# Column pairs in the simple recurrence, gate biases written by ScalarE, a new deal of the shared expert's tiles, in a four-layer recurrent kernel

## The chip, the cores and the metric

The kernel runs on one core of one Trainium2 chip. The metric is device time in microseconds, the median of several executions of the whole kernel. Before the change it is 1193.13 us (three runs, 1192.58 to 1193.31). Below, TensorE is PE in the rows of the profile, its weight loads are PEld, VectorE is DVE, ScalarE is ACT, GpSimd is POOL, and SyncE is SP (SPq for its queue of transfers).

## The reference

Four layers run in a row on x of shape (16, 256, 256), that is batch B, time T, width D. Each layer's output is added to its input. Only the first three matter here.

```python
# layer 0: a simple recurrence, h0 = cond
xW = einsum('ntd,dh->tnh', x, Wx) + b
h  = tanh(h @ Wh + xW[t])                      # for each of 256 times
x  = x + hs
# layer 1: an LSTM, h0 = cond, c0 = 0
hb = x[:, t] @ Wx + b + h @ Wh                 # 4 x 256 wide: i, f, o, g
c  = sigmoid(f) * c + sigmoid(i) * tanh(g)
h  = sigmoid(o) * tanh(c)
x  = x + hs
# layer 2: a shared expert for all, and two of four experts for each batch entry
x  = x + gelu(x @ sw1 + sb1) @ sw2 + sb2 + (routed experts, weighted)
# layer 3: a low-rank adapter, with weights made from cond
x  = x + adapter(x, cond)
```

## The kernel before

**Layout.** Activations are kept transposed: 128 partitions hold half of the width (C = 2 halves), the free dimension holds batch and time. Each product is done to nearly float32 accuracy with float16 operands: a value is split into a high part (HI) and a low part (LO), and three matmuls per pair of 128-blocks are summed in PSUM (helper `three`, lines 1132 to 1134): high weight times high data, low weight times high data, high weight times low data.

**Blocks and steps.** Time is cut into NB = 16 blocks of U = 16 steps. `block_steps(it, ...)` is written out once per engine. In block `it`, step `u` does the LSTM of time it*16+u, the simple recurrence of the next block at the same place, and a part of the shared expert for the block before (FILL, a table of tiles h, hidden, and d, down). So three layers run at the same time, one block apart. Before block 0 the simple recurrence runs alone for 16 steps. In blocks 1 to 8 (`matrix=True`) an eighth of the expert weights is split into high and low parts on the way (`weight_hi` on ACT, line 483; `weight_lo` on DVE, line 680; at the steps EXPERT_WINDOWS), and a part of the adapter's matrix is made (`low_rank` on PE, `low_hi` line 579 on ACT, `low_lo` line 902 on DVE, both in steps 14 and 15). After block 15 follow the routed experts and the adapter, which the change leaves almost alone.

**One step on PE.** First the LSTM's 48 matmuls of 16 columns (24 and 12 for the gates f, i, g, then 8 and 4 for o; lines 1229 and 1235). They wait for the state's high part (`v_hh`), and the last 12 of the first set for its low part (`v_hl`). Then the simple recurrence: 8 matmuls on the high part of its state (line 1203), 4 on the low part (line 1209). Then the input products of later steps for the LSTM: `fig_x` (64 columns) and `o_x` (128 columns), each tile with a bias matmul (line 1285) ahead of six others. Then the tiles that FILL names. At the end of a block `rnn_x`, 14 matmuls of 256 columns (line 1187 is its bias).

**One step on ACT.** `lstm_gates` (tfig, line 523, waits for f, i, g; to, line 527), then `rnn_step` (rf and RH, lines 517 and 518, the same tanh written as float32 and float16), then `lstm_cell` (tc, line 534), then the gelu of a hidden tile if the step has one (line 539), then the weight splits.

**One step on DVE.** `lstm_step`: fc, ig, c2 (lines 790, 791, 793), cell (795), then after tc the state's high part hh (797), h2 (800), the low part hl (802), and X (804). Then the longer work: `split_x2` (747, 750, 754), `split_g` (the cast at 777 and the difference at 779 for each gelu), `weight_lo`, and `split_x` (737 and 740), which makes the input XR of the simple recurrence two blocks ahead.

**One step on POOL.** The low part of the simple recurrence's state (line 396), and its sum with x (398 to 407).

Every engine takes its instructions in the order written here, and semaphores join them. The order is written by hand, nothing is planned at run time.

Of the kernel before, what the change touches and what calls it, by code (L numbers as in the profile page):

```python
# [22 lines left out]
ALU = mybir.AluOpType  # L23
# [34 lines left out]
def build_program(nc, a, out, scratch):  # L58
    ctx = ExitStack()
    with ctx:  # L60
# [25 lines left out]
        ones_pad = sb("ones_pad", [P, 256], F16)  # L86
        idf = sb("idf", [P, P], F32)
# [7 lines left out]
        rf = sb("rf", [P, 2, C, B], F32)  # L95
        x1s = sb("x1s", [P, 2, C, B], F32)
# [6 lines left out]
        cell = sb("cell", [P, C * B], F32)  # L103
# [52 lines left out]
        def late(*shape):  # L156
# [41 lines left out]
            a_xr p_xr pe_rx pe_r a_rh  p_rlo p_x1 p_x1h p_x1l  # L198
            pe_fig pe_o a_fig v_ig v_c2 a_tc v_hh v_h2 v_hl v_x2
# [37 lines left out]
        EXPERT_WINDOWS = (2, 4, 6, 8, 10, 12, 13, 14)  # L237
# [46 lines left out]
        def _(sp):  # L284
            with nc.allow_non_contiguous_dma(reason="small tables, once"):
# [22 lines left out]
                for quarter in range(4):  # L308
                    load_x(1, quarter)
                small_tables(sp)  # L310
# [68 lines left out]
        def _(pool):  # L379
# [9 lines left out]
            def rnn_step(blk, r):  # L389
# [80 lines left out]
        def _(act):  # L470
# [23 lines left out]
            nc.scalar.activation(XR[:, HI, 0].rearrange("p t b -> p b t"), X[:, 0, :, 0:U], ACT.Copy  # L494
# [40 lines left out]

            def gelu(tile, m, scale, bias, banks):
# [4 lines left out]


            piece = 0
            for r in range(U):
                rnn_step(0, r)
                for _ in range(LSTM_PIECES[r]):
# [5 lines left out]
            def block_steps(it, first, last, matrix=False):  # L552
                for u in range(U):
                    lstm_gates(it, u)
                    if not last:
                        rnn_step(it + 1, u)
                    lstm_cell(it, u)
                    if not first:
                        for kind, m in FILL[u]:
                            if kind == "h":  # L560
                                gelu(it * M + m, m, 1 / S_W1, sb1[:, m:m + 1], HB)
# [28 lines left out]
            for m in range(M):  # L590
                gelu(NB * M + m, m, 1 / S_W1, sb1[:, m:m + 1], HB)
# [63 lines left out]
        def _(dve):  # L655


            dve.sem_inc(s["v_gh"], M)
# [32 lines left out]
            V.memset(cell[:], 0.0).then_inc(s["v_const"], 1)  # L691
# [865 lines left out]
```

## Time and profile before

| what | value |
|---|---|
| median of 3 runs | 1193.13 us |
| the profiled execution's own time | 1185.64 us |
| its span, first to last instruction | 1183.8 us |
| PE busy, PEld busy | 1137.6 us (96%), 1028.1 us (87%) |
| DVE, ACT, POOL busy | 885.1 us (75%), 513.6 us (43%), 401.2 us (34%) |
| mean granted clock of TensorE | 0.968 of full speed |
| recurrences: block 0 to block 15 | from 50.6 us to 757.6 us of the span |

A row of the timeline gives an instruction's start and its duration, both in us. The durations of neighbours on one engine overlap, so what an instruction takes up of its engine's time is read as the distance between two starts where the second waits for nothing else. Busy time of PE is not PE at its peak, since matmuls are pipelined.

### The profile page before, as it was taken

Reading aid. Unit: us, or ns where it says so; the run is one execution under the profiler, and the core shown is the slowest. Engines: PE = TensorE matmul, PEld = TensorE weight load, DVE = VectorE, ACT = ScalarE, POOL = GpSimd, SP = SyncE. Lnnn points to the kernel's source line nnn. Section 1 sums busy time; section 2 is a strip of 40 time slices with the busy share of each in tenths; the row PEclk is TensorE's granted clock in tenths of the full one; section 3 lists DMA queues with packets and bytes.
Section 4 is the critical chain, followed back from the end, with each engine's and each line's share of the span. In section 5 each row is a group of like instructions: output and inputs, shape, how many; then the busy total and the mean of one; then the engine's idle time right before and its main releaser. Section 6 shows DMA issues by size and latency. Waiting matters only on the chain.

```text
span 1183.8 us, 58924 instructions
## 1 busy us (share of the span) xinstructions
PE 1137.6 (96%) x24138; PEld 1028.1 (87%) x24138; DVE 885.1 (75%) x3368; ACT 513.6 (43%) x1897; POOL 401.2 (34%) x1369
## 2 busy tenths in 40 slices
PE   4899999999999999999999999899999999999898
PEld 3789889889889899999999998778888888888777
DVE  6577888887887887787787778787666666666697
ACT  3344444454444444444444443433333333333476
POOL 2654454454454454554454441064000000000041
PEclk7758999999999999999999999899999999999999
DMA  8211202202112021110000000000000000000022
GB/s 244 74 39 44 79 5 80 71 13 79 29 54 80 11 73 26 16 16 11 4 4 5 4 4 4 2 1 2 2 2 2 1 2 2 2 2 2 3 77 86
DMA packets 43282, 37.17 MB, mean 31 GB/s; under 512 B 23128, under 2 KB 38794, under 8 KB 43020
## 3 DMA queue, kind: packets, MB, share of 16 engines
q1 hardware_dynamic: 42412, 33.12, 9.2%
q8 instruction: 197, 3.23, 1.1%
q14 instruction: 65, 0.53, 0.1%
q10 hardware_dynamic: 608, 0.30, 0.1%
HBM read 28.42 MB, written 4.98 MB: 28 GB/s over the span
## 4 chain that ended last, share of the span: by engine, by line
PE 86%; DVE 8%; ACT 2%; POOL 2%; issue 2%; DMA 1%; SPq 0%; POOLq 0%; DVEq 0%; ACTq 0%
PE bank L1132 17%; PE bank L1133 17%; PE bank L1134 17%; PE bank L1229 16%; PE bank L1235 8%; PE bank L1203 4%; PE bank L1209 2%; DVE seq L740 2%; PE bank L1285 1%; ACT tc L534 1%; DVE LH L797 1%; PE bank L1275 1%; PE bank L1500 1%; DMA XHL<-in_x 1%; PE bank L1472 1%
## 5 line engine op out<-in xcount | busy, mean ns | idle before, releaser
L1229 PE MATMUL bank<-LH,seq 128*128 128x16 f16 x8192 | 282.1, 170 | 12.3 <-DVE LH L797 10.7
L1229 PEld LDWEIGHTS bank<-LH,seq 128*128 128x128 f16 x8192 | 250.6, 96 | 44.0 <-DVE LH L797 32.1
L539 ACT ACTIVATE gel<-bank,seq 128x256 f32<-128x256 f32 x256 | 121.2, 474 | 215.7 <-PE bank L1134 215.5
L1132 PE MATMUL bank<-XHL,WE 128*128 128x256 f16 x768 | 210.3, 274 | 2.6 <-DVE XHL L763 2.1
L1132 PE MATMUL bank<-GH,WE 128*128 128x256 f16 x768 | 209.8, 273 | 2.6 <-DVE GH L779 2.3
L777 DVE CAST GH<-gel 128x256 f16<-128x256 f32 x384 | 123.6, 322 | 117.6 <-ACT gel L539 110.8
L1134 PE MATMUL bank<-XHL,WE 128*128 128x256 f16 x768 | 210.4, 274 | 0.0
L1133 PE MATMUL bank<-XHL,WE 128*128 128x256 f16 x768 | 210.3, 274 | 0.0
L1133 PE MATMUL bank<-GH,WE 128*128 128x256 f16 x768 | 209.7, 273 | 0.0
L1134 PE MATMUL bank<-GH,WE 128*128 128x256 f16 x768 | 209.6, 273 | 0.0
L523 ACT ACTIVATE tfig<-bank 128x96 f32<-128x96 f32 x256 | 63.8, 249 | 286.4 <-PE bank L1235 286.4
L1235 PE MATMUL bank<-LH,seq 128*128 128x16 f16 x4096 | 177.2, 169 | 1.6 <-issue 1.6
L779 DVE TENSOR_TENSOR GH<-gel,GH 128x256 f16<-128x256 f32 x384 | 168.2, 438 | 13.2
L396 POOL TENSOR_TENSOR RH<-rf,RH 128x32 f16<-128x32 f32 x256 | 64.1, 250 | 322.8 <-ACT RH L518 313.0
L1134 PE MATMUL bank<-seq 128*128 128x64 f16 (+2 forms) x960 | 145.5, 206 | 0.0
L1133 PE MATMUL bank<-seq 128*128 128x64 f16 (+2 forms) x960 | 144.6, 206 | 0.0
L1132 PE MATMUL bank<-seq 128*128 128x64 f16 (+2 forms) x960 | 143.7, 206 | 0.0
L1235 PEld LDWEIGHTS bank<-LH,seq 128*128 128x128 f16 x4096 | 139.1, 96 | 1.1 <-issue 1.1
L462 POOL TENSOR_TENSOR seq<-X,seq 128x512 f16<-128x512 f32 x16 | 21.8, 1367 | 336.1 <-ACT seq L600 336.1
L790 DVE SCALAR_TENSOR_TENSOR fc<-tfig,cell 128x32 f32<-128x32 f32 x256 | 52.1, 204 | 73.0 <-ACT tfig L523 69.6
L405 POOL TENSOR_TENSOR seq<-x1s,seq 128x32 f16<-128x32 f32 x256 | 86.3, 337 | 36.7
L407 POOL COPY X<-x1s 128x32 f32<-128x32 f32 x256 | 93.8, 366 | 0.3
(190 smaller groups left out, 2583.9 us busy)
## 6 DMA issues: line engine op xcount, KB each, us to landing
stage<-in_L_cond_ew SPq DMA_DIRECT2D x8, 1024.0 KB, 8.7
stage<-in_L_cond_W SPq DMA_DIRECT2D x8, 1024.0 KB, 6.1
XHL<-in_x SPq DMA_DIRECT2D x8, 512.0 KB, 9.0
out<-WE SPq DMA_DIRECT2D x16, 256.0 KB, 2.2
stage<-in_L_cond_sw SPq DMA_DIRECT2D x2, 1024.0 KB, 5.4
scratch<-rows SPq DMA_DIRECT2D x96, 8.0 KB, 2.3
stage<-in_L_cond_Wx SPq DMA_DIRECT2D x1, 1024.0 KB, 8.7
stage<-in_L_cond_Wh SPq DMA_DIRECT2D x1, 1024.0 KB, 10.8
```

The lines of the kernel that those rows point to most:

```text
L396: nc.gpsimd.tensor_tensor(RH[:, slot, LO], rf[:, slot], RH[:, slot, HI], ALU.subtract).then_inc(s["p_rlo"], 1)
L405: nc.gpsimd.tensor_tensor(xs[:, LO, :, r % G, :], x1s[:, slot], xs[:, HI, :, r % G, :], ALU.subtract).then_inc(s["p_x1l"], 1)
L407: nc.gpsimd.tensor_copy(x, x1).then_inc(s["p_x1"], 1)
L523: nc.scalar.activation(tfig[:], FIG[u // H % 2][:, 0:6 * H * B].rearrange("p (m t b) -> p m t b", m=6, t=H)[:, :, u % H, :], ACT.Tanh, sca ...
L539: nc.scalar.activation(gel[:, m % 2, :], banks[m % len(banks)][:, 0:256], ACT.Gelu_apprx_tanh, scale=scale, bias=bias).then_inc(s["a_g"], 1)
L777: V.tensor_copy(GH[:, m % 4, HI], gel[:, m % 2]).then_inc(s["v_gh"], 1)
L779: V.tensor_tensor(GH[:, m % 4, LO], gel[:, m % 2], GH[:, m % 4, HI], ALU.subtract).then_inc(s["v_gl"], 1)
L1132: MM(out_, w(HI), x(HI), start=start, stop=False, skip_group_check=True)
L1133: MM(out_, w(LO), x(HI), start=False, stop=False, skip_group_check=True)
L1134: return MM(out_, w(HI), x(LO), start=False, stop=stop, skip_group_check=True)
L1229: MM(z, LW[:, h, 1, c, tile * P:(tile + 1) * P], LH[:, old, HI, c], start=False, stop=False, skip_group_check=True)
L1235: last = MM(z, LW[:, HI, 1, c, tile * P:(tile + 1) * P], LH[:, old, LO, c], start=False, stop=(c == C - 1), skip_group_check=True)
```

## The change

- **Simple recurrence.** The bank RB is laid out anew: two groups of 8 steps follow each other in it, with two columns sets (a = 0 and 1) for each. High weights meet the pair of high and low state in one matmul of 32 columns, so a step has 4 matmuls of 16 columns and 4 of 32 columns in place of 12 of 16. A DVE reduction (`rnn_sum`, into the new tile rz) adds the two sets, and stands in `lstm_step` behind hl. ACT's rf and RH wait for it. `rnn_x` is done for 8 steps at a time, with matmuls of 128 columns, in steps 0 and 8.
- **Biases.** After the first two turns no bias matmul precedes `fig_x` and `o_x`. ACT writes the biases into PSUM (`seed`, 384 elements for f, i, g after each fourth step; 256 for o after each eighth) from a small table that eight more transfers load and POOL scales.
- **ACT's order.** tc comes before rf and RH; then seeds, gelu, the high part of XR (`x_hi`, formerly DVE's cast), weight splits.
- **Gelu.** ACT computes it twice, once as float32 (gel) and once as float16 (GH, HI). DVE's cast goes, and only the difference (`shared_lo`) stays.
- **XR.** It is read across and written along (before: read along, written across). X_HI = (9, 10) on ACT, X_LO = (10, 12) on DVE.
- **DVE.** The scaling into cell goes, c2 is kept and scaled inside the next product.
- **Deal.** FILL is dealt in halves of a tile, the number per step being HALVES. The tiles come ahead of `fig_x` in a step. `o_x` for the second half of a block is in steps 3 and 5. EXPERT_WINDOWS and SPLIT_WINDOWS move.

```diff
-        EXPERT_WINDOWS = (2, 4, 6, 8, 10, 12, 13, 14)
+        EXPERT_WINDOWS = (2, 3, 4, 5, 6, 8, 9, 11)
...
 # ACT
             def rnn_step(blk, r):
                 n = blk * U + r
-                z = RB[:, :].rearrange("p (m t b) -> p m t b", m=C, t=U)[:, :, r, :]
-                act.wait_ge(s["pe_r"], n + 1)
+                z = rz[:]
+                act.wait_ge(s["v_rz"], n + 1)
...
+            def seed(n_read, bank_, tiles, steps, done):
+                act.wait_ge(s["a_tc"], n_read)
+                n = (tiles.stop - tiles.start) * steps * B
+                act.wait_ge(s["p_gate_bias"], 3)
+                nc.scalar.activation(bank_[:, 0:n].rearrange("p (m t) -> p m t", t=steps * B),
+                                     gate_bias[:, tiles].rearrange("p (m o) -> p m o", o=1).to_broadcast(
+                                         [P, tiles.stop - tiles.start, steps * B]), ACT.Copy).then_inc(s[done], 1)
+            def seeds(it, u, last):
+                if u % H == H - 1 and not (last and u >= U - 2 * H):
+                    seed(it * U + u + 1, FIG[u // H % 2], slice(0, 6), H, "a_fig_seed")
+                if u % G == G - 1 and not last:
+                    seed(it * U + u + 1, OB[u // G], slice(6, 8), G, "a_o_seed")
+            def x_hi(blk, c):
+                act.wait_ge(s["pe_rx"], 2 * blk)
+                nc.scalar.activation(XR[:, HI, c], X[:, c, :, blk * U:(blk + 1) * U].rearrange("p b t -> p t b"),
+                                     ACT.Copy).then_inc(s["a_xr"], 1)
+            def shared_gelu(tile, m):
+                act.wait_ge(s["pe_h"], tile + 1)
+                act.wait_ge(s["v_gl"], tile - 1)
+                nc.scalar.activation(gel[:, m % 2, :], HB[m % 2][:, 0:256], ACT.Gelu_apprx_tanh,
+                                     scale=1 / S_W1, bias=sb1[:, m:m + 1])
+                act.wait_ge(s["pe_d"], tile - 3)
+                nc.scalar.activation(GH[:, m % 4, HI], HB[m % 2][:, 0:256], ACT.Gelu_apprx_tanh,
+                                     scale=1 / S_W1, bias=sb1[:, m:m + 1]).then_inc(s["a_g"], 1)
...
                 for u in range(U):
                     lstm_gates(it, u)
+                    lstm_cell(it, u)
                     if not last:
                         rnn_step(it + 1, u)
-                    lstm_cell(it, u)
+                    seeds(it, u, last)
...
 # DVE
+            def shared_lo(tile, m):
+                dve.wait_ge(s["a_g"], tile + 1)
+                V.tensor_tensor(GH[:, m % 4, LO], gel[:, m % 2], GH[:, m % 4, HI], ALU.subtract
+                                ).then_inc(s["v_gl"], 1)
+            def rnn_sum(n):
+                pair = RB[:, :].rearrange("p (a m t b) -> p m t b a", a=2, m=C, t=G)[:, :, n % G]
+                dve.wait_ge(s["pe_r"], n + 1)
+                V.reduce_sum(rz[:], pair, AX_X).then_inc(s["v_rz"], 1)
...
-                V.tensor_tensor(c2[:], fc[:], ig[:], ALU.add).then_inc(s["v_c2"], 1)
-                dve.wait_ge(s["v_c2"], n + 1)
-                V.tensor_scalar(cell[:], c2[:], 0.5, None, ALU.mult)
+                V.scalar_tensor_tensor(c2[:], fc[:], 0.5, ig[:], ALU.mult, ALU.add).then_inc(s["v_c2"], 1)
...
                 V.tensor_tensor(hl, h2[:], hh, ALU.subtract).then_inc(s["v_hl"], 1)
+                if rnn:
+                    rnn_sum(n + U)
...
 # PE
+                if r % G == 0 and n > 0:
+                    rnn_x(blk, r // G)
...
                 for m in range(C):
                     for c in range(C):
-                        for h in (HI, LO):
-                            MM(z[:, m, r], RW[:, h, 1, c, m * P:(m + 1) * P], RH[:, old, HI, c],
-                               start=False, stop=False, skip_group_check=True)
+                        MM(z[:, 0, m, r % G], RW[:, LO, 1, c, m * P:(m + 1) * P], RH[:, old, HI, c],
+                           start=False, stop=False, skip_group_check=True)
...
-                        last = MM(z[:, m, r], RW[:, HI, 1, c, m * P:(m + 1) * P], RH[:, old, LO, c],
+                        last = MM(z[:, :, m, r % G], RW[:, HI, 1, c, m * P:(m + 1) * P], RH[:, old, :, c],
                                   start=False, stop=(c == C - 1), skip_group_check=True)
...
-FILL = [[] for _ in range(U)]
-for _m in range(M):
-    FILL[max(2 * _m - 1, 1)].append(("h", _m))
-    FILL[min(2 * _m + 2, 14)].append(("d", _m))
+HALVES = [0, 3, 2, 2, 2, 2, 2, 3, 0, 3, 2, 3, 2, 3, 2, 1]
+O_STEPS = (3, 5)
...
+X_HI, X_LO = (9, 10), (10, 12)
-SPLIT_WINDOWS = (0, 0, 2, 12)
+SPLIT_WINDOWS = (0, 0, 3, 7)
```

The new FILL takes the halves in the order h0, then h1, d0, h2, d1, up to h7, d6, then d7. So a hidden tile is finished, and its gelu done, in steps 1, 2, 4, 6, 7, 10, 11 and 13.

## Rows read from the trace of the kernel before

**Rows 1.** The page: busy time by engine, its share of the span, instructions.

```profile
PE 1137.6 (96%) x24138; PEld 1028.1 (87%) x24138; DVE 885.1 (75%) x3368; ACT 513.6 (43%) x1897; POOL 401.2 (34%) x1369
```

**Rows 2.** Windows of blocks 0, 1, 9, 15: PE, PEld, DVE, ACT, POOL, clock, DMA.

```profile
50.60:95.30 44.70, 41.17 (x1175) 38.34 (x1173) 30.56 (x148) 19.14 (x96) 22.85 (x80) 0.58 0.14 42
95.30:140.90 45.60, 45.16 (x1311) 41.53 (x1309) 37.20 (x163) 22.03 (x97) 21.39 (x80) 1.00 0.08 27
...
460.90:504.00 43.10, 43.10 (x1273) 40.70 (x1270) 33.28 (x154) 18.45 (x88) 20.78 (x80) 1.00 0.13 15
...
717.80:757.60 39.80, 35.87 (x981) 31.53 (x978) 32.38 (x169) 13.51 (x53) 0.00 (x0) 1.00 0.02 3
```

**Rows 3.** Timeline of PE in block 8: start us, duration us, operation.

```profile
424.90 0.19 PE L1134 MATMUL bank<-seq 128*128 128x64 f16 x1
424.93 0.27 PE L1132 MATMUL bank<-XHL,WE 128*128 128x256 f16 x1
425.04 0.27 PE L1133 MATMUL bank<-XHL,WE 128*128 128x256 f16 x1
...
425.66 0.76 PE L1229 MATMUL bank<-LH,seq 128*128 128x16 f16 x24
426.27 0.45 PE L1235 MATMUL bank<-LH,seq 128*128 128x16 f16 x12
```

**Rows 4.** Timeline of ACT and DVE, the same step of block 8.

```profile
424.31 0.25 ACT L523 ACTIVATE tfig<-bank 128x96 f32<-128x96 f32 x1 [1.19 <-PE bank L1235]
424.59 0.19 DVE L790 SCALAR_TENSOR_TENSOR fc<-tfig,cell 128x32 f32<-128x32 f32 x1 [0.35 <-ACT tfig L523]
...
425.41 0.19 DVE L797 SCALAR_TENSOR_TENSOR LH<-to,tc 128x32 f16<-128x32 f32 x1
...
425.82 0.19 DVE L802 TENSOR_TENSOR LH<-h,LH 128x32 f16<-128x32 f32 x1
425.93 0.21 DVE L804 SCALAR_TENSOR_TENSOR X<-h,X 128x32 f32<-128x32 f32 x1
...
426.71 0.42 DVE L779 TENSOR_TENSOR GH<-gel,GH 128x256 f16<-128x256 f32 x1
426.75 0.25 ACT L523 ACTIVATE tfig<-bank 128x96 f32<-128x96 f32 x1 [0.49 <-PE bank L1235]
...
427.05 0.18 DVE L790 SCALAR_TENSOR_TENSOR fc<-tfig,cell 128x32 f32<-128x32 f32 x1
```

**Rows 5.** Timeline of ACT: pairs in which the second waits for nothing else.

```profile
452.13 0.47 ACT L539 ACTIVATE gel<-bank,sb 128x256 f32<-128x256 f32 x1 [0.41 <-PE bank L1134]
452.50 0.41 ACT L483 ACTIVATE WE<-stage 128x256 f16<-128x256 f32 x1
...
455.89 1.33 ACT L579 ACTIVATE rows<-low_f 128x256 f16<-128x256 f32 x1 [1.13 <-DVE low_f L896]
456.73 0.70 ACT L483 ACTIVATE WE<-stage 128x256 f16<-128x256 f32 x1
...
1165.25 0.62 ACT L600 ACTIVATE seq<-X 128x512 f16<-128x512 f32 x1
1165.77 0.65 ACT L635 ACTIVATE WE<-bank 128x256 f32<-128x256 f32 x2
```

**Rows 6.** Timeline of ACT's tfig in block 9: steps 3, 4, 15, next block.

```profile
469.28 0.25 ACT L523 ACTIVATE tfig<-bank 128x96 f32<-128x96 f32 x1 [1.48 <-PE bank L1235]
471.73 0.25 ACT L523 ACTIVATE tfig<-bank 128x96 f32<-128x96 f32 x1 [0.50 <-PE bank L1235]
...
499.99 0.25 ACT L523 ACTIVATE tfig<-bank 128x96 f32<-128x96 f32 x1 [2.16 <-PE bank L1235]
504.01 0.25 ACT L523 ACTIVATE tfig<-bank 128x96 f32<-128x96 f32 x1 [2.95 <-PE bank L1235]
```

**Rows 7.** Groups by line and shape, whole span: count, busy us, mean ns.

```profile
L740 DVE TENSOR_TENSOR seq<-X,seq 128x256 f16<-128x256 f32 x30 | 39.0, 1299 | 0.0
...
L754 DVE TENSOR_REDUCE blocksum<-X 128x16 f32<-128x256 f32 x32 | 13.0, 411 | 0.0
```

More of the change, by code:

```diff
@@ L309, in _ @@
                     load_x(1, quarter)
+                for i, tile in enumerate(FIG_TILES + O_TILES):
+                    sp.dma_start(gate_bias[:, i:i + 1], a["L1_cond_b"][tile * P:(tile + 1) * P].rearrange("(p o) -> p o", o=1)
+                                 ).then_inc(s["ld_gate_bias"], 16)
                 small_tables(sp)
@@ L821, in _ @@
             for r in range(U):
+                rnn_sum(r)
                 for _ in range(LSTM_PIECES[r]):
@@ L913, in block_steps @@
                                 split_x2(it - 1, k)
-                        for kind, m in FILL[u]:
-                            if kind == "h":
-                                split_g(it * M + m, m)
+                        for kind, m, halves in FILL[u]:
+                            if kind == "h" and C - 1 in halves:
+                                shared_lo(it * M + m, m)
                     for i in SHARED_PIECES[u] if first else ():
@@ L1237, in lstm_step, with hidden, down_, shared_hidden @@
                     last.then_inc(s[done], 1)
[L1239 to L1242 removed]
+            def hidden(tile, w, x, bank_, free, halves=range(C)):
+                if 0 in halves:
+                    free()
+                for c in halves:
                     last = three(bank_[:, 0:256], lambda h: w(h, c), lambda h: x(h, c), c == 0, c == C - 1)
[L1244 to L1249 removed]
+                if C - 1 in halves:
+                    last.then_inc(s["pe_h"], 1)
+            def down_(tile, j, w, first, last_, ybank, halves=range(C)):
+                if 0 in halves:
+                    pe.wait_ge(s["v_gl"], tile + 1)
+                for c in halves:
                     last = three(ybank[:, c * 256:(c + 1) * 256], lambda h: w(h, c),
                                  lambda h: GH[:, j % 4, h], first and c == 0, last_)
[L1252 to L1254 removed]
+                if C - 1 in halves:
+                    last.then_inc(s["pe_d"], 1)
+            def shared_hidden(blk, m, halves=range(C)):
                 tile = blk * M + (M + m)
@@ L1353, in spread_logits, with block_steps @@
                    skip_group_check=True).then_inc(s["pe_gate"], 1)
-            def block_steps(it, first, last, rx, matrix=False):
+            def block_steps(it, first, last, matrix=False):
                 for u in range(U):
@@ L1363, in block_steps @@
                         logits()
+                    if not first:
+                        for kind, m, halves in FILL[u]:
+                            if kind == "h":
+                                shared_hidden(it - 1, m, halves)
+                            else:
+                                shared_down(it - 1, m, halves)
                     if u == 0:
@@ L1514, in _, with fill_table @@
             adapter_steps(pe, step)
-FILL = [[] for _ in range(U)]
-for _m in range(M):
-    FILL[max(2 * _m - 1, 1)].append(("h", _m))
-    FILL[min(2 * _m + 2, 14)].append(("d", _m))
+HALVES = [0, 3, 2, 2, 2, 2, 2, 3, 0, 3, 2, 3, 2, 3, 2, 1]
+O_STEPS = (3, 5)
+def fill_table():
+    jobs = [("h", 0)] + [job for m in range(1, M) for job in (("h", m), ("d", m - 1))] + [("d", M - 1)]
+    stream = [(kind, m, c) for kind, m in jobs for c in range(C)]
+    table, at = [], 0
+    for n in HALVES:
+        step = {}
+        for kind, m, c in stream[at:at + n]:
+            step.setdefault((kind, m), []).append(c)
+        table.append([(kind, m, tuple(cs)) for (kind, m), cs in step.items()])
+        at += n
+    assert at == len(stream)
+    return table
+FILL = fill_table()
 N_SCRATCH = 16 * Q * C * 3 * 4
```

171 lines of the change are left out of this document (80 added, 91 removed).

## The prediction

> **What bounds the kernel now.** I read the page first, then windows by block, then the timeline inside one step. The page has PE busy for 96% of the span [rows 1], and the windows show where that is so: block 9 is PE from end to end, 43.1 of 43.1 us, while DVE has 33.3 us of work in it and ACT 18.4 [rows 2]. ACT looks free.
>
> The starts of neighbouring matmuls give PE's prices at the full clock: 24 matmuls of 16 columns take 0.61 us, so 0.025 each; one of 64 columns 0.03 (0.0285 over longer runs); one of 256 columns 0.11 [rows 3]. For 128 columns I take 0.056, half of the 256. A step of before costs PE 48 + 12 matmuls of 16 columns (1.50 us), plus for `fig_x` 0.20 per tile, plus 0.66 per tile of the shared expert. By that, steps 3, 5, 7 and so on with one hidden tile and one `fig_x` tile cost 2.35 us, and step 15 with `o_x`, `rnn_x` and a `fig_x` tile 1.50 + 0.20 + 0.78 + 1.53 = 4.0. The starts of tfig in block 9 show 2.45 for step 3 and 4.02 for step 15 [rows 6]. So the long steps are PE's work, and the short ones stand at 2.45, above PE's 2.35.
>
> That 2.45 is the second bound, the LSTM's own loop. From tfig, in one step: fc at 0.28, the state's high part at 1.10 to 1.29, its low part hl at 1.51, X at 1.62, PE's next LSTM matmuls at 1.35, next tfig at 2.44 [rows 3, 4]. A block of 16 steps can't be shorter than 16 x 2.44 = 39.0 us, whatever PE has to do.
>
> **The change on PE.** Matmuls of 32 columns: no row has one, it lies between 0.025 (16 columns) and 0.0285 (64), and I take 0.025. The simple recurrence falls from 12 to 8, 0.10 us a step, 1.6 a block (1.54 at the other bound). The bias matmuls that go are 6 x 4 of 64 columns and 4 of 128: 0.91 a block. `rnn_x` costs 28 x 0.056 = 1.57 in place of 14 x 0.11 = 1.53. With the new deal, PE's work W per step is 1.40, plus 0.78 for `rnn_x` in steps 0 and 8, plus 0.327 per half, 0.17 per `fig_x` tile, 0.33 per `o_x` tile. It comes out at 2.40 in the even steps 2, 4, 6, 10, 12, 14 and 2.52 to 2.57 in the others, 39.7 us a block, against 42.4 before (43.1 measured with the short steps raised to 2.45). In blocks 1 to 8 `low_rank` adds 1.14.
> The Trainium skill (TensorE: Matmul & The Clock Gate, Back-to-back issue gap) gives some 25 ns from start to start for anything up to 64 columns. The trace agrees at 16 columns with 0.025, and by the page 32 columns cost the same.
>
> **The change on ACT, step by step.** rf and RH now wait for `rnn_sum`, which stands behind hl on DVE. It starts where X started, 1.62 after tfig. It is a reduction of 64 elements to 32; the nearest rows are the 32-element operations at 0.19 [rows 4] and the reduction of 256 at 0.41 [rows 7], and I take 0.21. So rf can't start before 1.87. RH follows 0.09 later and whatever comes next 0.08 after that, at 2.05. All the rest that ACT has in the step, seeds, gelus, `x_hi`, weight splits, is queued behind it, and behind all that waits the next tfig, wanted at 2.44. From tc to 1.87 ACT stands idle with this work behind the waiting instruction. The room left for it is 0.39, or 0.50 where PE's W of 2.55 sets the step.
> The Trainium skill (PSUM — Partial Sum Buffer, Engine vs sequencer instructions) says that the queues of ScalarE and VectorE are strictly first in, first out. The trace agrees: ACT sits idle for 1.19 us ahead of a tfig [rows 4].
>
> What has to go into that room, as distances between starts: a gelu takes 0.37 [rows 5], and two of them 0.74; a copy of 256 elements takes between 0.27 and 0.37 there, 512 take 0.52 [rows 5], so I take 0.30 for a weight split or an `x_hi`, 0.40 for the seed of 384 elements (bounds 0.27 and 0.52) and 0.27 for the one of 256. `x_hi` reads across; the old layout, which wrote across, cost DVE 1.30 [rows 7], and that is its upper bound.
>
> A gelu step therefore makes the next tfig late by 0.74 - 0.39 = 0.35. DVE adds to it: `shared_lo` waits for the second gelu's end at 2.05 + 0.37 + 0.47 = 2.89, starts at 2.92 and gives DVE back 0.34 later (426.71 to 427.05 in [rows 4]) at 3.26, while fc is wanted at 2.79 + 0.28 = 3.07. Lateness 0.19 more. The next state is late by the sum, PE waits, and the interval that follows a gelu step is 2.44 + 0.35 + 0.19 = 2.98, where PE needs 2.40 or 2.55. Where the step before was PE's, at 2.55, it is 2.86.
>
> The intervals of steps 0 to 15 in blocks 9 to 14 by this rule, each the larger of W and 2.44 plus the lateness: 2.58, 2.55, 2.86, 2.97, 2.44, 2.97, 2.44, 2.97, 3.64, 2.55, 2.44, 3.39, 3.37, 2.55, 2.86, 2.57. Step 8 is the longest because step 7 has both seeds and a gelu pair, 0.40 + 0.27 + 0.74 = 1.41. Step 11 follows a gelu pair with `x_hi` (1.04) and `x_lo` behind it on DVE, step 12 a seed and a pair (1.14), step 0 both seeds. Sum 45.15 against 43.1: +2.05 a block.
>
> In blocks 1 to 8 each weight split adds 0.30 on ACT, and `weight_lo`, 0.34 on DVE, waits for it at the end of the queue. Four of the eight stand in gelu steps (2, 4, 6, 11). The same rule gives 3.29, 2.55, 2.86, 3.30, 2.92, 3.30, 2.56, 3.30, 3.64, 2.55, 2.72, 3.39, 3.70, 3.12, 2.44, 3.24 (step 15 follows `low_hi`, 0.84 by [rows 5]; steps 12 and 13 carry `low_rank`). Sum 48.9 against 45.6 [rows 2]: +3.3.
>
> **What costs nothing, and its cover.** The cast of gel, the cell product and the casts and scattered writes of XR leave DVE, some 9.6 us a block by its rows, and 16 reductions come (3.4): DVE has 33.3 of 43.1 us and was not the bound, so this gives nothing but shorter lateness, which is counted above. Eight transfers of 512 bytes stand ahead of the small tables in SP's queue; they are early in the kernel, the first load behind them waits for weight splits anyway, and if that cover failed they would cost 1 to 2 us once. POOL's three scalings fall between blocks, POOL has 20.8 of 43.1 us.
>
> **Start and end.** `rnn_x(1)`, 3 us at half clock, leaves the path before block 0, and `rnn_x(2)` its end, but 1.5 comes back in each stage, the 16 lone steps get the reduction (+0.25 less 0.12 of matmuls each) behind weight splits and copies on DVE, and block 0 (clock 0.58 [rows 2]) has seeds and `x_hi` in the way of tfig. I take +2.5 for both stages, between -4 and +8. Block 15 has no rf and RH, so ACT is free after tc: -0.8; in the tiles behind it eight casts less: -0.5.
>
> **The sum.** 8 x 3.3 = 26.4; 6 x 2.05 = 12.3; +2.5; -1.3. That is +39.9 us. The profiled execution took 1185.6 us with a span of 1183.8, the median of the three runs is 1193.1, 0.6% more; the sum is a difference of 1225.5 to 1185.6, and set upon the median it gives 1233.
>
> **Rivals.**
> *PE's work comes through.* If ACT's queue never holds up tfig (the sum of the pair is ready early, or the two gelus take less than half), the blocks go down to W: -3.4 in blocks 9 to 13, -1.9 in 14, -4.1 in 1 to 8 (their waits for loads stay), -3 at the start: about -55, 1138. For it: PE is at 96% and ACT at 43% [rows 1]. Against: rf's place behind hl and the gelus' place behind rf are in the program, and 0.74 doesn't fit in 0.39. It decides from the point where a pair and what stands with it take less than 0.4 to 0.5. The Trainium skill (Perfetto Trace Analysis, Identifying the Most-Contended Engine) would optimise the engine with the highest occupancy first, here PE with its weight loads at 87%; by that page alone this rival is the forecast. Chance 0.17.
> *Half hidden.* If the second gelu and the copies follow at 0.27, the lower bound of [rows 5], a pair overruns by 0.24, and each of eight intervals is 0.1 to 0.2 shorter, those with seeds and splits 0.3: 43.2 to 43.6 in blocks 9 to 14 and 46.5 to 47 in 1 to 8, so +10 to +15: about 1206. Chance 0.15.
> *The clock falls.* PE gets gaps of 0.4 to 0.6 us in seven or eight steps of a block and of 1 us in step 8, which has no tile. In block 0, without tiles, the granted clock was 0.58 [rows 2]. At half clock a step's tiles and input products would take twice their time, about +1 us a step in the stretches concerned; two steps a block in 14 blocks add 28: about 1260. Against it: block 15, PE busy for 35.9 of 39.8 us, kept 1.00 [rows 2]. Chance 0.08.
> *The forecast*, ACT's queue behind the pair sum: 0.60, with its own range 1216 to 1250.
>
> **How the numbers follow.** A measurement of this kernel tells some 0.2% from no change, 2.4 us. Faster comes from the first rival and a little of the second: 0.19. Slower: 0.76. Within 0.2%: 0.05, the lower edge of the second. The range of 8 in 10 leaves out the first rival and the far side of the clock's: 1190 to 1258.
>
> **What the changed profile would show.** The idle time ahead of rf is put down to DVE's reduction, about 0.8 us a step; tfig is no longer released by PE in about half of the steps; PE's wait for the state's high part (line 797 before) grows from some 0.1 to about 5 us a block; PE busy falls below 90% in blocks 1 to 14; the intervals of tfig alternate between 2.44 to 2.57 and about 3, with the longest, 3.6, after step 7. Block 9 takes 45 us, a matrix block 49. The prediction is wrong if tfig's intervals are all 2.4 to 2.57, if the reduction starts well before hl ends, or if two gelus start less than 0.3 apart.

## The result, and the profile after

The changed kernel takes 1261.34 us (median of 4 runs, 1258.69 to 1263.24) against 1193.22 us before (4 runs): ratio 1.0573, 95% interval 1.0555 to 1.0591. It is slower by 68 us, where 40 were forecast, and lies 3 us above the forecast's range. The profiled execution took 1259.87 us with a span of 1258.1 and a mean granted clock of 0.953.

The page of the kernel after, the line of engines (busy us, share, count), answers to [rows 1]:

```profile
PE 1135.2 (90%) x22906; PEld 1016.8 (81%) x22906; DVE 788.8 (63%) x3210; ACT 597.7 (48%) x2147; POOL 381.4 (30%) x1372
```

Every engine but ACT has no more work than before, and the span is longer. So the time went into waiting. The windows of blocks 0, 1, 9 and 15, same columns as [rows 2]:

```profile
53.60:101.00 47.40, 39.08 (x1111) 36.85 (x1108) 28.30 (x146) 23.23 (x105) 20.57 (x78) 0.57 0.12 40
101.00:151.60 50.60, 45.17 (x1213) 41.15 (x1211) 30.40 (x153) 27.01 (x115) 20.73 (x80) 0.95 0.10 31
508.00:554.90 46.90, 42.51 (x1191) 39.40 (x1189) 27.46 (x145) 23.38 (x106) 19.64 (x82) 1.00 0.12 15
787.90:826.80 38.90, 35.00 (x949) 31.79 (x949) 27.30 (x145) 17.12 (x64) 0.62 (x3) 0.99 0.01 4
```

Block 9 takes 46.9 us where it took 43.1, and PE is busy for 42.5 of it, not for all. Only block 15, which has no simple recurrence, is shorter, 38.9 against 39.8. The table of waits of the kernel after (engine, what waits, what for: us in total, times, longest):

```profile
ACT rf L525 <- DVE rz L832: 194.2, 256, 2.9
ACT tc L542 <- DVE c L847: 161.3, 256, 1.6
...
PE bank L1281 <- DVE LH L849: 78.3, 135, 1.6
...
ACT tfig L531 <- PE bank L1287: 38.6, 79, 3.7
```

and two rows of the same table of the kernel before:

```profile
ACT tfig L523 <- PE bank L1235: 286.4, 248, 5.3
...
PE bank L1229 <- DVE LH L797: 10.7, 32, 0.9
```

Before, ACT waited for PE at nearly every tfig. Now it does so 79 times, and PE waits for the state: 78 us in place of 11. What stands between is the first row, rf waiting for the pair sum in each of 256 steps. One gelu step of block 9, timeline of ACT, DVE and POOL (start, duration):

```profile
525.32 0.25 ACT L531 ACTIVATE tfig<-bank 128x96 f32<-128x96 f32 x1 [0.31 <-PE bank L1287]
...
525.52 0.26 POOL L404 TENSOR_TENSOR seq<-X,rf 128x32 f16<-128x32 f32 x1
525.61 0.22 DVE L844 SCALAR_TENSOR_TENSOR fc<-tfig,c 128x32 f32<-128x32 f32 x1 [0.84 <-ACT tfig L531]
...
525.92 0.24 POOL L409 TENSOR_TENSOR seq<-x1s,seq 128x32 f16<-128x32 f32 x1
525.97 0.25 DVE L847 SCALAR_TENSOR_TENSOR c<-fc,ig 128x32 f32<-128x32 f32 x1
...
526.84 0.19 DVE L854 TENSOR_TENSOR LH<-h,LH 128x32 f16<-128x32 f32 x1
526.95 0.22 DVE L832 TENSOR_REDUCE rz<-bank 128x32 f32<-128x64 f32 x1
...
527.20 0.23 ACT L525 ACTIVATE rf<-rz 128x32 f32<-128x32 f32 x1 [0.72 <-DVE rz L832]
527.34 0.21 ACT L526 ACTIVATE RH<-rz 128x32 f16<-128x32 f32 x1
527.46 0.46 ACT L575 ACTIVATE gel<-bank,sb 128x256 f32<-128x256 f32 x1
...
527.81 0.46 ACT L578 ACTIVATE GH<-bank,sb 128x256 f16<-128x256 f32 x1
...
528.17 0.25 ACT L531 ACTIVATE tfig<-bank 128x96 f32<-128x96 f32 x1
...
528.31 0.43 DVE L816 TENSOR_TENSOR GH<-gel,GH 128x256 f16<-128x256 f32 x1 [1.02 <-ACT GH L578]
```

This is the step of the forecast: the pair sum (rz) starts 1.63 after tfig; rf starts at 1.88, after ACT has stood idle for 0.72; the two gelus start at 2.14 and 2.49, and the next tfig at 2.85, with no wait of its own. A second thing wasn't forecast. c2 (the profile writes it c) takes 0.25 and fc 0.22, beside POOL's operations. Before the change fc took 0.19 [rows 4], and so did c2 in the same step of block 8, on the timeline of DVE:

```profile
424.92 0.19 DVE L793 TENSOR_TENSOR c<-fc,ig 128x32 f32<-128x32 f32 x1
```

The chain of tfig starts in block 13 shows what a pair of steps costs, steps 3 to 5 and the next:

```profile
703.48 0.25 ACT L531 ACTIVATE tfig<-bank 128x96 f32<-128x96 f32 x1
...
706.23 0.24 ACT L531 ACTIVATE tfig<-bank 128x96 f32<-128x96 f32 x1
...
709.07 0.25 ACT L531 ACTIVATE tfig<-bank 128x96 f32<-128x96 f32 x1
...
711.80 0.25 ACT L531 ACTIVATE tfig<-bank 128x96 f32<-128x96 f32 x1 [0.31 <-PE bank L1287]
```

The interval of a step runs here from its own tfig to the next one; the prediction's lists count the same interval under the step that it ends in. Steps 4 and 5, one with a gelu and one without, take 2.84 + 2.73 = 5.57. The whole block takes 46.43.

Where the time went, from the tfig starts of the two traces (the stages begin at 51.7, 96.3, 460.9, 717.8 before and at 53.6, 101.0, 508.0, 787.9 after): start stage +1.9, block 0 +2.8, blocks 1 to 8 +42.4, blocks 9 to 14 +23.0, block 15 -0.95, all behind it +5.1. The last lies in the final 89 us (84 before), where the granted clock was 0.92 against 0.98; no run tests it. The profiled executions differ by 74 us, the medians by 68, because the profiled execution before was 8 us faster than its median.

### The profile page after: what moved, and what is told of

The parts are those of the page before. It is cut to its first block and busy times, and to the rows that moved or that the text cites. A ratio compares the mean times of both kernels' runs of the same rounds, so it can differ in the third digit from the quotient of the medians.

```text
span 1258.1 us, 56828 instructions
## 1 busy us (share of the span) xinstructions
PE 1135.2 (90%) x22906; PEld 1016.8 (81%) x22906; DVE 788.8 (63%) x3210; ACT 597.7 (48%) x2147; POOL 381.4 (30%) x1372
## 5 line engine op out<-in xcount | busy, mean ns | idle before, releaser
L1281 PEld LDWEIGHTS bank<-LH,seq 128*128 128x128 f16 x8192 | 242.6, 96 | 113.4 <-DVE LH L849 105.9
L525 ACT ACTIVATE rf<-rz 128x32 f32<-128x32 f32 x256 | 58.7, 229 | 194.2 <-DVE rz L832 194.2
L1183 PE MATMUL bank<-seq 128*128 128x64 f16 (+1 forms) x1024 | 148.7, 205 | 0.0
L1182 PE MATMUL bank<-seq 128*128 128x64 f16 (+1 forms) x1024 | 147.4, 205 | 0.1
L1181 PE MATMUL bank<-seq 128*128 128x64 f16 (+1 forms) x1024 | 145.9, 205 | 0.6 <-POOL seq L409 0.6
L823 DVE CAST GH<-gel 128x256 f16<-128x256 f32 x256 | 78.3, 306 | 104.0 <-ACT gel L569 103.1
L1287 PEld LDWEIGHTS bank<-LH,seq 128*128 128x128 f16 x4096 | 139.4, 96 | 0.0
L542 ACT ACTIVATE tc<-c 128x32 f32<-128x32 f32 x256 | 58.7, 229 | 161.3 <-DVE c L847 161.3
L470 POOL TENSOR_TENSOR seq<-X,seq 128x512 f16<-128x512 f32 x16 | 19.2, 1205 | 342.3 <-ACT seq L644 342.3
L1181 PEld LDWEIGHTS bank<-seq 128*128 128x128 f16 x1024 | 99.7, 101 | 3.5 <-POOL seq L409 0.7
```

Of the source, the lines that this page charges most:

```text
L525: nc.scalar.activation(rf[:, r % 2], z, ACT.Tanh, scale=1 / S_RNN)
L542: nc.scalar.activation(tc[:], c2[:], ACT.Tanh, scale=0.5).then_inc(s["a_tc"], 1)
L823: V.tensor_copy(GH[:, m % 4, HI], gel[:, m % 2]).then_inc(s["v_gh"], 1)
L1181: MM(out_, w(HI), x(HI), start=start, stop=False, skip_group_check=True)
L1182: MM(out_, w(LO), x(HI), start=False, stop=False, skip_group_check=True)
L1183: return MM(out_, w(HI), x(LO), start=False, stop=stop, skip_group_check=True)
```

## The experiments

The kernel before was run on the same chips: 1191.38 us in the first group of four runs below, 1191.69 in the second, 1190.36 in the third, 1188.97 in the last three. Ratios are to it. The kernel before varies by some 4 us between these chips and that of the first measurement (1188.97 to 1193.22), so a small difference to the changed kernel's 1261.34 us is better read from the ratios.

**1. The sum ahead of the state.** `rnn_sum` moves on DVE from behind hl to between c2 and hh.

```diff
                 V.scalar_tensor_tensor(c2[:], fc[:], 0.5, ig[:], ...)
+                if rnn:
+                    rnn_sum(n + U)
                 dve.wait_ge(s["a_tc"], n + 1)
...
                 V.tensor_tensor(hl, h2[:], hh, ALU.subtract)
-                if rnn:
-                    rnn_sum(n + U)
```

> The changed kernel with one thing moved: DVE does the pair sum between c2 and the state's high part, where it waits for tc anyway. Queue theory (rf and RH late behind hl, everything else of ACT late behind them): rf starts about 1.1 us after tfig in place of 1.89, the room for seeds, gelus and splits grows from 0.39 to about 1.2 us, tfig is again released by PE in nearly every step, blocks 9 to 13 fall from 46.6 to about 40 us, blocks 1 to 8 from 50.8 to about 42, in all about 1261 - 100 = 1160, faster than before (1193). Rival (ACT's added work is too much wherever it stands, or the sum delays the state): blocks stay above 43 us, 1200 to 1250. Second rival (the reductions in steps 0 and 8 hold up the state because PE does rnn_x ahead of the recurrence): two steps a block 0.3 us longer, 9 us in all of the gain.

1172.89 us, ratio 0.9844 (0.9817 to 0.9871): 88 us less than the changed kernel, and 1.6% faster than the one before. The blocks fell less than expected, 9 to 14 to 41.3 us on average (expected 40) and 1 to 8 to 45.0 (expected 42), so the 1160 expected wasn't reached. One gelu step of its block 13, timeline:

```profile
632.95 0.25 ACT L531 ACTIVATE tfig<-bank 128x96 f32<-128x96 f32 x1 [0.87 <-PE bank L1287]
...
633.67 0.22 DVE L832 TENSOR_REDUCE rz<-bank 128x32 f32<-128x64 f32 x1
...
633.92 0.23 ACT L525 ACTIVATE rf<-rz 128x32 f32<-128x32 f32 x1
...
634.53 0.46 ACT L578 ACTIVATE GH<-bank,sb 128x256 f16<-128x256 f32 x1
...
635.39 0.25 ACT L531 ACTIVATE tfig<-bank 128x96 f32<-128x96 f32 x1 [0.40 <-PE bank L1287]
```

rf starts at 0.97 in place of 1.88, the gelu pair is over at 2.04, and tfig waits for PE again, as it does 187 times in this run. The place of one operation of 0.22 us decides the sign of the change.

**2. One gelu.** DVE casts gel again, ACT computes one gelu.

```diff
+                V.tensor_copy(GH[:, m % 4, HI], gel[:, m % 2]).then_inc(s["v_gh"], 1)
...
-                nc.scalar.activation(GH[:, m % 4, HI], HB[m % 2][:, 0:256], ACT.Gelu_apprx_tanh, ...)
```

> The changed kernel with one gelu per tile on ACT and the cast back on DVE. If the second gelu is the cause by itself: each of eight intervals a block 0.5 us shorter, about 1261 - 50 = 1210. Queue theory: ACT's part goes (0.37 fits in the room of 0.39), but the cast and the difference on DVE now follow the late gelu, end 0.4 to 0.5 us after fc is wanted and take its place; only 0.05 to 0.1 us a gelu step is won, 1248 to 1256.

1259.53 us, ratio 1.0583 (1.0554 to 1.0613), no change; not even the small gain expected came. ACT's lateness of 0.35 went, and DVE's cast took its place, as its timeline shows:

```profile
705.83 0.30 DVE L815 CAST GH<-gel 128x256 f16<-128x256 f32 x1 [0.65 <-ACT gel L575]
706.16 0.43 DVE L817 TENSOR_TENSOR GH<-gel,GH 128x256 f16<-128x256 f32 x1
706.59 0.19 DVE L845 SCALAR_TENSOR_TENSOR fc<-tfig,c 128x32 f32<-128x32 f32 x1
```

tfig had started at 705.74, so fc comes at 0.85, not 0.28. Behind a late rf the work holds up the loop on whichever engine it stands.

**3. POOL later.** POOL waits for the next c2 before its last four operations of a step.

```diff
+                if n >= U:
+                    pool.wait_ge(s["v_c2"], n - U + 2)
```

> The changed kernel with one more wait on POOL: after the low part of the simple recurrence's state it waits for the next LSTM step's c2 before its four other operations, which nothing needs soon. All intervals of tfig are 0.1 us longer than the 2.44 of the loop before, in steps without any work of ACT too; in block 15, where POOL does nothing, they are 2.44. Contention theory (POOL's operations now run beside fc and c2, before they ran beside h2): fc falls from 0.218 to 0.19 us, c2 from 0.25 to 0.19, the shortest intervals from 2.63 to 2.55, 1.3 us a block, about 1261 - 18 = 1243. Rival (the longer loop is the form of c2 and the added wait ahead of fc): nothing changes or it gets slower, 1260 or more.

1273.84 us, ratio 1.069 (1.0658 to 1.0722), slower. fc, ig and c2 did fall to 0.19, and the step behind a gelu from 2.73 to 2.64. But x's sum now comes late for PE's input products at the start of each block, and they stand ahead of the LSTM's matmuls. The timeline of PE:

```profile
712.85 0.20 PE L1183 MATMUL bank<-seq 128*128 128x64 f16 x1 [0.84 <-POOL seq L411]
```

The interval of step 0 grew from 2.48 to 3.28. So the time of this run can't decide for or against the contention, and the gain of 18 us expected didn't come.

**4. Cell product back on DVE.** c2 is the plain sum again, and the scaling into cell returns.

```diff
-                V.scalar_tensor_tensor(c2[:], fc[:], 0.5, ig[:], ALU.mult, ALU.add)
+                V.tensor_tensor(c2[:], fc[:], ig[:], ALU.add)
+                V.tensor_scalar(cell[:], c2[:], 0.5, None, ALU.mult)
```

> The changed kernel with the cell product back on DVE, c2 a plain sum again and no wait ahead of fc. Rival of the contention theory: the loop falls by 0.1 us a step, about 1240. Contention theory: fc, ig and c2 keep their longer durations, the cell product stands where DVE waits for tc, so within 3 us of 1261.

1263.72 us, ratio 1.0597 (1.0561 to 1.0633), no change, and fc and c2 stay long. Their new form isn't the cause.

**5. Biases on PE.** No seeds on ACT, the bias matmuls return.

```diff
-                    seeds(it, u, last)
```

> The bias matmuls stand on PE again and ACT's seeds are gone; the sum of the pair stays behind hl. Theory (ACT's queue behind the pair sum holds up tfig): the interval after step 7 falls from 3.77 to about 3.05, step 11's from 3.3 to 2.9, step 15's from 2.85 to about 2.65, and PE's extra 0.91 us a block falls mostly into its gaps. That is -1.2 to -1.4 us a block in 15 blocks: about 1241 us (1236 to 1246). Rival (PE's work sets the blocks, the seeds are hidden in ACT's idle time): +0.5 to +0.9 a block, 1269 to 1275 us.

1240.68 us, ratio 1.0417 (1.0393 to 1.0442), 19 to 21 us less, as the theory had it. A seed behind a late rf costs more than the bias matmuls that it saves.

**6. rf and RH last on ACT.** The sum stays behind hl. ACT does seeds, gelus, copies and splits first.

```diff
                     lstm_cell(it, u)
-                    if not last:
-                        rnn_step(it + 1, u)
                     seeds(it, u, last)
...
+                    if not last:
+                        rnn_step(it + 1, u)
```

> ACT does rf and RH after the seeds, the gelu pair, the copy of XR and the weight splits; the sum of the pair stays behind hl on DVE. Theory (what costs is work queued behind the waiting rf, not the sum's place in itself): a gelu pair starts at about 1.2 after tfig and is over at 1.95, rf then starts where its sum lets it anyway, and tfig comes on time. The intervals fall to 2.54 to 2.65, the one after step 7 to 2.8: blocks 9 to 14 to about 42.3 us, the kernel to about 1195 us (1180 to 1210). Rival (the sum's place behind hl, so the late state of the simple recurrence, costs by itself, or two gelus are too much for ACT anywhere): 1240 us or more.

1189.23 us, ratio 0.9973 (0.9956 to 0.9991): 72 us back without touching DVE. Timeline of ACT in its block 13:

```profile
645.07 0.25 ACT L531 ACTIVATE tfig<-bank 128x96 f32<-128x96 f32 x1 [0.31 <-PE bank L1287]
...
646.14 0.46 ACT L575 ACTIVATE gel<-bank,sb 128x256 f32<-128x256 f32 x1
646.49 0.47 ACT L578 ACTIVATE GH<-bank,sb 128x256 f16<-128x256 f32 x1
646.95 0.23 ACT L525 ACTIVATE rf<-rz 128x32 f32<-128x32 f32 x1
...
647.61 0.25 ACT L531 ACTIVATE tfig<-bank 128x96 f32<-128x96 f32 x1 [0.31 <-PE bank L1287]
```

rf is no earlier than in the changed kernel (1.88), yet the next tfig, 2.54 after the first, waits for PE and for nothing on ACT. So it is not the late state of the simple recurrence that cost, but what stood behind the waiting instruction. The Trainium skill (PSUM — Partial Sum Buffer, Engine vs sequencer instructions) calls these queues strictly first in, first out; runs 1 and 6, which change an order and nothing else, agree with 88 and 72 us. (The prediction's own sign for it, ACT idle for 1.19 ahead of a tfig, shows a wait and not yet an order.) Run 6 stays 16 us behind run 1, 15 of them in blocks 1 to 8 (375.3 us against 360.1); what costs them wasn't tested.

**7. Early sum and biases on PE**, the edits of 1 and 5.

> The sum of the pair between c2 and the state (as in the run with 1172.9 us), and the biases on PE again. With the queue free PE is what is left: its 0.91 us a block come back, less some 0.2 at steps 7 and 8 where the seeds still held ACT: +0.7 a block in 15 blocks, about 1183 us (1179 to 1188). If the seeds on ACT are worth nothing also now: 1172 us. If they cost more than the matmuls: below 1170 us.

1179.26 us, ratio 0.9888 (0.9864 to 0.9912). With the queue free the seeds are worth 5 to 6 us, little more than the noise (the intervals of this run and run 1 just overlap); with it blocked they cost 19 to 21.

**8. Early sum and one gelu**, the edits of 1 and 2.

> The sum of the pair between c2 and the state, and one gelu with DVE's cast again. The cast (0.34 us) starts behind X at about 1.75 after tfig and the difference is over at about 2.5, ahead of the next fc at 2.72; ACT was idle anyway. So no change against 1172.9 us: 1170 to 1176. If DVE's time is what the second gelu buys: 1180 us or more.

1175.66 us, ratio 0.9855 (0.9807 to 0.9902), the same as run 1 within the intervals. The second gelu buys nothing that these runs tell.

**9. No pairs.** 12 matmuls of 16 columns, no sum, rf and RH read PE's bank; all else as changed.

```diff
-                z = rz[:]
-                act.wait_ge(s["v_rz"], n + 1)
+                z = RB[...][:, 0, :, r % G]
+                act.wait_ge(s["pe_r"], n + 1)
```

> All of the change but the column pairs: 12 matmuls of 16 columns again, no sum on DVE, rf and RH read PE's bank. Theory (the whole loss comes from rf waiting behind DVE's sum): rf starts at about 0.9 to 1.1 after tfig, the gelu pair and the seeds fit, and the blocks fall to PE's work, which is 0.10 us a step more than with pairs: blocks 9 to 14 at 41.3 to 42 us, about 1185 us (1178 to 1192). Rival (the second gelu, the seeds or the new deal cost by themselves): 1220 us or more.

1177.50 us, ratio 0.9882 (0.9848 to 0.9917). All of the change but the pairs gains; the pairs with their sum behind hl turn that into the loss of 68. Against run 1 the pairs are worth only about 5 us, within the intervals. Two parts are hidden in that: the first tfig comes at 46.5 without pairs and at 53.6 in run 1, and from there to the last tfig it is 700.8 us without them and 690.3 in run 1. So the pairs gain some 10 us in the blocks and lose some 7 ahead of them.

**10. Small POOL.** From block 0 on POOL's last four operations of a step cover one column each, so this kernel leaves out the rest of the simple recurrence's sum with x.

```diff
+                    nc.gpsimd.tensor_tensor(x1[:, one], x[:, one], h[:, one], ALU.add)
...
-                nc.gpsimd.tensor_tensor(x1, x, h, ALU.add)
```

> The kernel after the change with the four later operations of POOL's step cut to one column each from block 0 of the LSTM on (x1s, both parts of seq, X), so the sum of the simple recurrence with x is left out for all but that column. Theory (the loop of 2.54 in place of 2.44 is DVE's fc, ig and c2 slowed beside POOL's operations): fc, ig and c2 take 0.18 to 0.19 again, the steps after a gelu step fall from 2.73 to 2.64 and blocks 9 to 14 from 46.4 to 45.0 us: about 1238 us (1234 to 1243). Rival (the 0.1 us is from something else, such as the new order of ACT or the new form of c2): 1257 us or more.

1247.45 us, ratio 1.0475 (1.0438 to 1.0513): 14 us less than the changed kernel (12 by the ratios), between the two theories. Groups by line of the kernel after (total us, mean ns of one), then of this one:

```profile
L844 DVE SCALAR_TENSOR_TENSOR fc<-tfig,c 128x32 f32<-128x32 f32 x256 | 54.3, 212 | 56.4 <-ACT tfig L531 53.7 <-issue 1.2
...
L847 DVE SCALAR_TENSOR_TENSOR c<-fc,ig 128x32 f32<-128x32 f32 x256 | 52.6, 206 | 8.8
```

```profile
L859 DVE SCALAR_TENSOR_TENSOR c<-fc,ig 128x32 f32<-128x32 f32 x256 | 49.2, 192 | 8.9
...
L856 DVE SCALAR_TENSOR_TENSOR fc<-tfig,c 128x32 f32<-128x32 f32 x256 | 48.0, 187 | 59.6 <-ACT tfig L543 58.1 <-issue 1.2
```

The durations fall as expected, and steps 4 and 5 of block 13 take 2.75 + 2.65 = 5.40. The prediction's rule gives 2.79 + 2.63 = 5.42 for such a pair. So with the contention gone the rule is right to 0.02 for this pair. From fc to tc it is now 0.54 to 0.57 in nearly every step. But the block takes 45.47, not 45.0, and block 4 49.63 where 48.9 was forecast.

**11. Early sum, even deal.** HALVES = [0, 4, then twelve times 2, 4, 0].

> The sum of the pair between c2 and the state, and the shared expert's halves dealt as before the change: 0, 4, twelve times 2, 4, 0. PE's work by the prices of the prediction grows in step 8 by 0.65, in step 14 by 0.60 and in step 1 by 0.32, and falls in steps 7, 9, 11, 13, 15 by 0.10 each to the loop: +1.1 us a block in 15 blocks, about 1189 us (1180 to 1195). Rival (the deal does not matter, gaps take it up): 1173 us.

1178.02 us, ratio 0.9897 (0.9861 to 0.9934). The deal is worth 5 us of the 16 expected, and the intervals of this run and run 1 overlap. A block of the late ones takes 41.8 against 41.0. Step 14 grew by 0.62 as expected, but step 8 by 0.30 and not by 0.65, since in run 1 it stood above PE's work already (2.67).

**12. Early sum, later seed.** The seed for o moves from steps 7 and 15 to steps 8 and 0.

> The sum of the pair between c2 and the state, and the seed of 256 elements for o one step later, in the steps 0 and 8, which have no gelu. Theory (ACT's queue is what still holds up tfig after steps 7 and 15): the intervals of steps 7, 8 and 0 fall by 0.1 to 0.25 each, 0.5 us a block, about 1166 us (1162 to 1170). Rival (PE sets these steps): 1172 us.

1169.12 us, ratio 0.9809 (0.9773 to 0.9846). The interval of step 7 fell from 2.66 to 2.56, that of step 8 rose from 2.67 to 2.76, and blocks 10 to 14 take the same 41.0 as in run 1. The difference to run 1 is within the intervals, and the 0.5 us a block expected didn't come: the rival, that PE sets these steps, fits.

**13. Lone steps without pairs**, on top of 12: in the 16 steps ahead of block 0, 12 matmuls of 16 columns and no sum.

> The kernel with the early sum and the later seed, but in the 16 lone steps of the simple recurrence 12 matmuls of 16 columns and rf and RH straight from PE's bank, as in the run without pairs, whose first tfig came at 46.4. Theory (in the start stage the sum queues behind weight splits and copies on DVE, and that costs 6 to 7 us): first tfig at 46.5 to 47.5 and the rest unchanged, 1162 us (1160 to 1165). Rival (the load of the weights or the work of ACT sets the start of the LSTM, and the early tfig of that run is luck): 1168 us or more.

> The kernel with the early sum and the later seed once more, as the measure for the run without pairs in the lone steps: 1169 us (1167 to 1171).

1161.30 us against 1170.04 for the kernel of run 12 on the same chip: ratios 0.9764 (0.9734 to 0.9793) and 0.9841 (0.9808 to 0.9873). Timeline of ACT in the start stage, with the sum, then without:

```profile
30.52 0.23 ACT L525 ACTIVATE rf<-rz 128x32 f32<-128x32 f32 x1 [1.29 <-DVE rz L834]
32.46 0.23 ACT L525 ACTIVATE rf<-rz 128x32 f32<-128x32 f32 x1 [1.28 <-DVE rz L834]
...
52.82 0.25 ACT L531 ACTIVATE tfig<-bank 128x96 f32<-128x96 f32 x1 [3.75 <-PE bank L1289]
```

```profile
33.42 0.20 ACT L529 ACTIVATE rf<-bank 128x32 f32<-128x32 f32 x1 [0.96 <-PE bank L1270]
34.60 0.20 ACT L529 ACTIVATE rf<-bank 128x32 f32<-128x32 f32 x1 [0.59 <-PE bank L1270]
...
45.46 0.25 ACT L535 ACTIVATE tfig<-bank 128x96 f32<-128x96 f32 x1 [3.95 <-PE bank L1298]
```

In these lines a lone step takes 1.94 us with the sum and 1.18 without; over all 15 intervals of the stage the mean is 1.87 and 1.44. This is the fastest kernel of the study, 28 us below the one before on that chip.

**14. Small x_hi.** On the changed kernel, ACT's copy of XR covers one column from the third block on.

> The kernel after the change with ACT's copy of XR cut to one column from the third block on (the simple recurrence's input is left out but for it). Theory (the copy takes 0.54 us of ACT's queue, not 0.30, and all of it lies between rf and tfig): in blocks 9 to 14 step 9 falls from 2.67 to 2.57 and step 10 from 3.27 to 2.84, in blocks 1 to 8 each by 0.3 to 0.5: 8 to 10 us in all, 1251 to 1253 us. By the 0.30 of the prediction it would be 5 us, 1256. Rival (DVE's low part behind it holds the next fc anyway): 1259 us or more.

1257.17 us, ratio 1.0571 (1.0534 to 1.0607): by the ratio no change. The expected 1251 to 1253 us didn't come. In blocks 9, 10 and 12 the intervals of steps 9 and 10 fell from 2.67 to 2.56 and from 3.28 to 2.92, and that of step 11 rose from 3.32 to 3.78; in block 13 steps 10 and 11 did the same (2.85 and 3.76). The timeline of DVE in block 13 shows why:

```profile
725.94 0.42 DVE L820 TENSOR_TENSOR GH<-gel,GH 128x256 f16<-128x256 f32 x1 [1.02 <-ACT GH L582]
726.28 0.58 DVE L783 TENSOR_TENSOR seq<-X,seq 128x256 f16<-128x256 f32 x1
726.78 0.18 DVE L848 SCALAR_TENSOR_TENSOR fc<-tfig,c 128x32 f32<-128x32 f32 x1
```

`x_lo` now stands ahead of fc, which comes 0.88 after tfig. Most of the time goes from one queue to the other, as the rival of this run has it.

## Why the prediction was right and where it was not

**What bounds, and PE's part.** Right. Matmuls of 32 columns start 0.025 apart (four take 0.10), as this timeline of PE shows, and 9 of the 15 intervals of block 15 are at the loop, 2.44 to 2.47.

```profile
525.54 0.25 PE L1261 MATMUL bank<-RH,seq 128*128 128x32 f16 x4
525.64 0.27 PE L1181 MATMUL bank<-XHL,WE 128*128 128x256 f16 x1
```

PE's share fell to 87% in blocks 1 to 8, as forecast, but to 92% in blocks 9 to 14, where less than 90% was.

**ACT's queue behind the pair sum.** Right, and shown three ways: by moving the sum (run 1), by moving rf (run 6), by taking the sum away (run 9). The forecast rf at 1.87 reads 1.88.

**The lateness on DVE behind `shared_lo`.** Right: 0.19 forecast, and fc at 0.48 in place of 0.28 in the steps behind a gelu.

**What failed** is the size of one term, the sum of the intervals, "each the larger of W and 2.44 plus the lateness". It gave +3.3 us a block in blocks 1 to 8 and +2.05 in 9 to 14; measured are +5.3 (50.9 us a block, where 48.9 were forecast) and +3.8 (46.65, where 45.15 were). Blocks 1 to 8 lost 42.4 us where 26.4 were forecast, blocks 9 to 14 23.0 where 12.3 were, 27 us more together. The forecast is a sum upon the profiled execution before, and against that 74 us were lost, not 40. Of these 34 us missed, 27 are the blocks', 2 those of the start, and nearly 6 lie behind block 15 (+5.1 where -0.5 was forecast), with a cause that stays open. The parts of the 27:

- The loop of 2.44 was taken over from before, and nothing was put down for what else moves with rf. rf moved from 0.6 to 1.88 after tfig, so POOL's operations that follow it fall beside fc, ig and c2 of the next step, which carry the loop. Before, they fell beside h2 (its mean was 255 ns before and is 185 after), where they held up no tfig: hl behind it was over at 1.70, and its matmuls start at 1.96 [rows 3, 4]. From fc to tc it was 0.54 to 0.56 in 203 of the 224 steps of blocks 1 to 14; now it is 0.60 to 0.73 in 125 of them. Run 10 gives 12 to 14 us for POOL's part. The prediction asked only whether POOL has time enough (20.8 of 43.1 us), and not beside what its work would stand.
- The room of 0.39 on ACT was 0.30 to 0.32. RH follows rf by 0.13 and the next operation by 0.12, where 0.09 and 0.08 were taken from before; then both read PE's bank, now they read rz. In part the gelu's 0.35 (for 0.37) makes up for it, and run 10's pair of steps came out right.
- `x_hi` takes 0.54, not the 0.30 of a plain copy (start of it to tfig in step 9 of block 13, 723.17 to 723.71). Step 9 was forecast at 2.72 and takes 3.16 in a matrix block. Run 14 shows that taking it away alone brings nothing, so no number of us can be put against it.
- The rest: run 10 takes 5.2 us away in blocks 1 to 8 and 5.4 in 9 to 14. Of the other 16, 5 are in blocks 9 to 14 (nearly 2 of them because the blocks of before average 42.8, not the 43.1 of block 9) and 11 in blocks 1 to 8: step 0 at 2.92 where 2.55 was forecast, step 9 as above, steps 12 and 13 at 2.66 + 3.24 where 3.12 + 2.44 were, and steps of 4.0 and 4.4 in blocks 2 and 5 (in the latter PE stands idle for 1.62 with no releaser in the profile). These were read, not tested apart, and their causes stay open.

**The start stage and block 0** cost 4.7 us where 2.5 were taken for both stages, within the bounds of -4 to +8. The share of the sum was undersized: +0.13 a lone step forecast, 28.0 - 21.6 us over 15 of them = 0.43 measured (rf starts at 21.16 to 49.17 after, 24.26 to 45.84 before). In run 9, with all of the change but the pairs, the same 15 intervals take 21.9. Run 13 puts 9 us on it. rf started 3.1 us earlier than before, the 3 us forecast for `rnn_x`, and that hid it.

**The rivals.** *PE's work comes through* would have given 1138. With the queue free (run 1) PE's share is 95%, and tfig waits for PE 187 times. But blocks 10 to 14 are 41.0 against a W of 39.7, blocks 1 to 8 are 45.0 against the 41.5 of the rival, and the kernel stands at 1173. So that number was too good by 35 us even where its condition is nearly met. *Half hidden*: the second gelu follows at 0.35, not at 0.27, and run 2, without it, is no faster. *The clock falls* played a small part at most: in blocks 1 to 14 the mean granted clock was 0.99; before, it was 1.00.

## What to carry to other kernels

When an instruction is made to wait for a later one, list what is queued behind it on its engine, and move either the wait or the queue; here the place of an operation of 0.22 us was worth 88 us. And follow the shift one engine further: the operations that the delayed one releases land beside others than before, and their price in the loop no longer holds. A part of a change can only be priced once the queue is free: the seeds cost some 20 us with it blocked and gave 5 to 6 with it free.

## What the runs showed of the hardware

- DVE operations of 32 elements slow down beside POOL's: c2 from 0.19 to 0.25, and the slowed one changes with the place of POOL's work (h2 at 0.26 before and in run 3, hl at 0.26 in run 1, fc and c2 after). Both operands of these lie in SBUF. The Trainium skill (SBUF — State Buffer, Who interferes with whom) says that a VectorE instruction with two SBUF inputs contends with a GpSimd instruction that reads SBUF, and calls the port pair that they share an exclusive lock. The trace agrees on which instructions suffer, but these take only 0.03 to 0.08 us more, beside POOL operations of 0.24 to 0.26. In the step shown fc starts at 525.61, inside POOL's operation from 525.52 to 525.78, and is over at 525.83; with a full block until POOL is done it would be over 0.19 after 525.78, at 525.97.
- ACT's tanh of 32 elements takes 0.20 from PE's bank and 0.23 from rz, both in the kernel of run 13. The Trainium skill (Perfetto Trace Analysis, Optimizing Scalar/DVE Operations) gives ScalarE some 93 ns of overhead on SBUF and 51 on PSUM, 0.04 us apart; the distance from rf to RH, 0.09 and 0.13, differs by the same.
- The subtraction for XR's low part takes 0.59 us when it reads across and writes along, 1.30 when it reads X along and writes across [rows 7]. Groups by line of the kernel after:

```profile
L779 DVE TENSOR_TENSOR seq<-X,seq 128x256 f16<-128x256 f32 x30 | 17.8, 594 | 0.0
```
